# One matmul for mean and variance, and later places for residual, final addition, points and pooled copies

## The chip, the cores and the metric

The kernel runs on one core of a Trainium2 chip. A core has five engines that run side by side, each with its own stream of instructions in order: TensorE (PE, matrix products and transposes), VectorE (DVE, elementwise work and sums), ScalarE (ACT, activations and copies), GpSimd (POOL, which here only issues gathers) and SyncE (SP, which here only issues other transfers). They meet through semaphores: an instruction waits until a counter has reached a number. The metric is the time of one execution on the device in microseconds (us); lower is better.

## What is computed

Two residual layers on a batch of 16 images of 64 channels and 64x64 pixels, all in float32. `_gn` is a group norm with 32 groups, so each group is a pair of channels.

```python
x = x + _L0_conv_ref(_gn(x), ...)   # layer 0
x = x + _L1_conv_ref(_gn(x), ...)   # layer 1

# layer 0: a depthwise convolution whose kernels are made from the image itself
xh = _conv1x1(x, w_in, b_in)                       # 64 -> 128 channels
pooled = jnp.mean(xh, axis=(2, 3))
hcx = jax.nn.relu(pooled @ kg_w1.T + kg_b1)
kernels = (hcx @ kg_w2.T + kg_b2).reshape(b, c, K, K)
y = conv_general_dilated(x_r, k_r, ...)            # 3x3, one kernel for each channel
y = y * jnp.tanh(jax.nn.softplus(y))
return _conv1x1(y, w_out, b_out)                   # 128 -> 64 channels

# layer 1: a deformable 3x3 convolution
offset = _conv2d(x, w_off, b_off)
mask = jax.nn.sigmoid(_conv2d(x, w_mask, b_mask))
xd = _deform_conv(x, offset, mask, w_def)          # 9 taps, each bilinear over 4 corners
cat = jnp.concatenate([xd, offset, mask], axis=1)
z = jnp.einsum('bihw,oi->bohw', cat, w_1x1[:, :, 0, 0]) + ...
return jax.nn.silu(z * inv + ...)                  # batch norm, then silu
```

## The kernel before

**Groups and taps.** The 4096 pixels of an image are worked off in 8 groups of 512 (here "group 0" to "group 7"; the code's `g`). In each group the deformable convolution has 9 taps (`k`). For each tap GpSimd issues 4 gathers that fetch the four corners of 512 points from a table in DRAM (`patch_table`) into a slot of `gat`; VectorE multiplies the slot by its weights (L1096) and adds the four corners (`add_corners`, L1081); TensorE transposes the sums of two taps at a time into `tap_ps` (`transposes`, L545, "pair 0" to "pair 3", and the single ninth tap); ScalarE copies them to `val` (L801); TensorE multiplies them by the weights into `z_ps` (`product`, L553 and L555); ScalarE applies the silu (L810, into `zs`, a part of the tile `n_z`); and VectorE adds the input (`finish`, L1107), whose result SyncE stores (`store_out`). GpSimd may run ahead by less than a group: before taps 0, 2, 4, 6 and 7 it waits for the transposes of the group before (`THROTTLE`), and before each group for its indices `ixu` (L777).

**What goes on beside it.** While image b is gathered, layer 0 of image b+1 and the head of layer 0 of image b+2 are computed in the gaps. Groups 0 to 3 hold the depthwise convolution of b+1 on VectorE (`convolve 0` to `2`, L968 and L971), exp, ln and tanh on ScalarE, and in the following group the 1x1 product `project` (on VectorE L981, on TensorE L464) and the addition of x (`residual`, L995). Group 4 holds both group norms: the one of b+2 (`x_mean`, `x_var`, `x_norm`) with its way to the nine kernel values (`hidden_units`, `kernels`, ending in `kb`, L934), and the one of b+1 (`group_mean`, `group_var`, `normalise`). Groups 5 and 6 make the table and the offsets of b+1 (`to_table`, `offsets`, `to_pixels`; most of it on TensorE, then ScalarE), and group 7 makes the points, indices and corner weights from them (`points 0` to `2`, L1037 to L1057, and `next_indices`), and `hidden 0` to `3` of b+2 (VectorE normalises x into `n_z`, L898; TensorE multiplies by `w_in`, L442; ScalarE copies into `xh`, L689).

**What sets the order.** No scheduler: tuples called PLAN_... give, for each kind of group, pairs of a number and a step. `group()` runs the taps up to that number and then the step, and the same plan is walked by TensorE, ScalarE and VectorE, each with its own function of that name. So (4, "residual") means: after tap 3, on each engine that has a residual step. KK is 9, the end of the group. PLAN_FIRST is group 0, PLAN_BLOCK0 groups 1 to 3, PLAN_NORM group 4, PLAN_PREPARE groups 5 to 7, and PLAN_START the first three groups of the first image. Since every stream is in order, a step that waits holds up all that stands behind it on its engine.

**The lines that the change touches.** The variance of a pair of channels is made from the two channels' own means and variances: TensorE averages the means (L404, L468, one column), VectorE squares the deviation and adds the channel's own variance (L920, L1008), TensorE averages that (L409, L472), and ScalarE takes the root (L670, L726). After group 7 stood `finish(b, NCH - 1)`, outside any plan. Two loads of x stand in SyncE's stream at an image's end and the next one's start (L283).

## Time and profile before

| | us |
|---|---|
| median of 3 runs | 6700.41 |
| lowest and highest | 6698.43, 6706.16 |
| the profiled execution | 6738.33 |
| its span | 6736.5 |
| one image in steady state (image 7) | 418.8 |

The times are those of the whole execution. The profile is of one other execution, 38 us (0.6%) longer than the median. Times on the trace count from the span's start. A row of a timeline gives start, duration, engine, line, operation, tiles (written <- read), shapes, how many instructions are merged, and in brackets how long the engine had been idle before it and what ended that ("remote" and "issue" stand where the profile can't name the one that released it). A matmul in float32 shows as two records. The ends of TensorE's records are modelled, so when a product was really there is read from the engine that waited for it.

### The profile page before, as it was taken

To read this page: it belongs to the slowest core of one execution; us is meant where nothing else is said; L and a number is where in the kernel's file an instruction comes from. 1 tells how busy PE (TensorE), PEld (TensorE's weight loads), DVE (VectorE), ACT (ScalarE), POOL (GpSimd) and SP (SyncE) were. 2 spreads that over 40 slices of the span, in tenths; PEclk is the share of its full clock that TensorE was granted. 3 is DMA by queue.
4 is the path that set the end of the run, shared out by engine and by line. 5 is a ranking of instruction groups with operands and counts; after the bars stand their busy time and mean duration, and the time that the engine had idled before them with its cause. 6 is when DMAs were issued, how large, how long until landed. Compare 5 with 4: busy or idle time off the path is not lost.

```text
span 6736.5 us, 27541 instructions
## 1 busy us (share of the span) xinstructions
PE 3015.6 (45%) x7284; PEld 1087.0 (16%) x7284; DVE 5001.0 (74%) x4373; ACT 1678.4 (25%) x2375; POOL 4385.1 (65%) x4614
## 2 busy tenths in 40 slices
PE   7454353634535344363443635436353353534422
PEld 3121121211112111121111212112121111211100
DVE  5967769587686877768768696776958769587555
ACT  3332222322222222232222222222232222222200
POOL 2666666666666666666666666666666666666666
PEclk8775575755657566575665756657575576756655
DMA  3233343333433333333333333334333343333332
GB/s 90 91 103 113 93 122 96 104 109 97 116 94 105 106 102 113 94 105 110 103 109 96 105 111 101 112 94 119 98 100 112 96 119 94 106 100 103 100 99 88
DMA packets 306947, 695.25 MB, mean 103 GB/s; under 512 B 79172, under 2 KB 148580, under 8 KB 304548
## 3 DMA queue, kind: packets, MB, share of 16 engines
q0 software_dynamic: 221184, 604.27, 29.6%
q1 hardware_dynamic: 85606, 89.22, 5.3%
q8 instruction: 57, 0.93, 0.1%
q14 instruction: 100, 0.82, 0.0%
HBM read 639.06 MB, written 54.12 MB: 103 GB/s over the span
## 4 chain that ended last, share of the span: by engine, by line
DVE 38%; another core or an unknown queue 21%; issue 14%; PE 13%; POOL 7%; ACT 6%; DMA 0%; DVEq 0%; ACTq 0%; POOLq 0%; SPq 0%
DVE pairs L1081 11%; DVE gat L1096 9%; DVE conv_ps L971 8%; POOL gat L381 7%; PE conv_ps L519 3%; PE z_ps L553 2%; PE yo_ps L519 2%; DVE single L1081 1%; PE tap_ps L545 1%; DVE xb L995 1%; DVE stat L997 1%; DVE stat L908 1%; DVE conv_ps L968 1%; DVE uc L974 1%
## 5 line engine op out<-in xcount | busy, mean ns | idle before, releaser
L381 POOL DMA_INDIRECT gat<-patch_table,ixu x4608 | 4377.5, 950 | 2334.9 <-issue 1355.2
L1081 DVE TENSOR_REDUCE pairs<-gat 128x256 f32<-128x1024 f32 x1024 | 1935.3, 1890 | 0.0
L1096 DVE TENSOR_TENSOR gat<-gat,wgt_ps 128x1024 f32<-128x1024 f32 x1152 | 1395.1, 1214 | 515.8 <-DMA gat<-patch_table,ixu 471.6
L545 PE MATMUL tap_ps<-ident,pairs 128*128 128x128 f32 x2048 | 498.3, 388 | 2086.7 <-DVE pairs L1081 1358.9
L553 PE MATMUL z_ps<-val,w_pair 128*64 128x512 f32 x1024 | 895.1, 972 | 680.2 <-ACT val L801 457.4
L801 ACT ACTIVATE val<-tap_ps 128x512 f32<-128x512 f32 x512 | 304.1, 596 | 2742.2 <-remote 1446.5
L545 PEld LDWEIGHTS tap_ps<-ident,pairs 128*128 128x128 f32 x2048 | 329.3, 195 | 2519.1 <-DVE pairs L1081 1569.5
L971 DVE SCALAR_TENSOR_TENSOR conv_ps<-xh,kb,conv_ps 128x1024 f32<-128x1024 f32 x480 | 617.6, 1287 | 12.7
L519 PE MATMUL conv_ps<-np,w_om 128*41 128x512 f32 x732 | 384.0, 681 | 0.0
L519 PE MATMUL yo_ps<-np,w_om 128*41 128x512 f32 x804 | 370.1, 611 | 17.1 <-ACT omc L757 10.2
L555 PE MATMUL z_ps<-cat,w_last 105*64 105x512 f32 x256 | 194.0, 851 | 222.1 <-ACT cat L805 140.7
L553 PEld LDWEIGHTS z_ps<-val,w_pair 128*64 128x64 f32 x1024 | 136.9, 190 | 837.6 <-ACT val L801 487.8
L1081 DVE TENSOR_REDUCE single<-gat 128x256 f32<-128x1024 f32 x128 | 242.8, 1897 | 0.0
L810 ACT ACTIVATE n_z<-z_ps,bn_shift,bn_scale 64x512 f32<-64x512 f32 x128 | 99.0, 774 | 536.7 <-remote 353.6
L1037 DVE TENSOR_TENSOR pt<-px,grid 128x576 f32<-128x576 f32 (+2 forms) x20 | 12.8, 639 | 279.2 <-issue 245.6
L1107 DVE TENSOR_TENSOR n_z<-n_z,xb 64x512 f32<-64x512 f32 x128 | 86.5, 676 | 160.3 <-ACT n_z L810 121.5
L805 ACT ACTIVATE cat<-tap_ps 64x256 f32<-64x256 f32 x256 | 96.7, 378 | 384.4 <-remote 238.7
L898 DVE TENSOR_SCALAR n_z<-xb,mr 64x512 f32<-64x512 f32 x128 | 71.0, 580 | 140.5 <-remote 79.2
L981 DVE TENSOR_TENSOR uc<-uc,conv_ps 128x1024 f32<-128x1024 f32 x60 | 73.0, 1216 | 113.8 <-issue 113.8
L528 PE MATMUL xh_ps<-ident,omc 41*128 41x41 f32 x504 | 54.8, 268 | 215.5 <-ACT omc L759 213.4
L442 PE MATMUL xh_ps<-n_z,w_in 64*128 64x512 f32 x120 | 113.4, 1043 | 81.1 <-issue 45.9
L519 PEld LDWEIGHTS yo_ps<-np,w_om 128*41 128x41 f32 x804 | 94.8, 120 | 272.2 <-issue 254.6
(181 smaller groups left out, 3153.8 us busy)
## 6 DMA issues: line engine op xcount, KB each, us to landing
gat<-patch_table,ixu POOLq DMA_INDIRECT x4608
xb<-in_x SPq DMA_DIRECT2D x31, 1024.0 KB
patch_table<-rec SPq DMA_DIRECT2D x120, 256.0 KB
out<-n_z SPq DMA_DIRECT2D x128, 128.0 KB
patch_table<-np SPq DMA_DIRECT2D x2, 1072.5 KB
patch_table<-gat SPq DMA_DIRECT2D x8, 256.0 KB
patch_table<-rec_l SPq DMA_DIRECT2D x16, 97.0 KB
xb<-in_x SPq DMA_DIRECT2D x2, 512.0 KB, 5.1
```

The lines of the kernel that those rows point to most:

```text
L381: pool.indirect_dma_start(gat[:, slot, t * 2 * REC:(t + 1) * 2 * REC], None, table_rows, bass.IndirectOffsetOnAxis(ixu[:, i, k, t:t + 1], ...
L442: pe.matmul(hidden_ps(n, j)[:, :], w_in[C:, :], n0[C:, j, :], start=True, stop=True).then_inc(xh_mm, 1)
L519: m = pe.matmul((om_ps, yo_ps)[j][0:OM, :], w_om[:, i, :], inner(np1, 0, 128, c * ROWS + 2 * (i // 3), i % 3), start=(i == 0), stop=(i == 5))
L545: m = pe.transpose(tap_ps[p % 2][:, t * 128:(t + 1) * 128], pairs[:, p, t, :] if p < PAIRS else single[:, t, :], ident[:, :])
L553: pe.matmul(z_ps[0:C, :], w_pair[:, p, :], val[:, p % 2, :], start=(p == 0), stop=False).then_inc(z_mm, 1)
L555: pe.matmul(z_ps[0:C, :], w_last[:, :], cat[0:C + OM, b % 2, span(g)], start=False, stop=True).then_inc(z_mm, 1)
L801: act.activation(val[:, p % 2, :], tap_ps[p % 2][:, :], ACT.Copy).then_inc(tap_done, 1)
L805: act.activation(cat[0:C, b % 2, span(g)].rearrange("p (t h x) -> p t h x", h=2, x=128)[:, :, h, :], tap_ps[PAIRS % 2][C * h:C * h + C, 0: ...
L810: act.activation(zs[:, :], z_ps[0:C, :], ACT.Silu, bias=bn_shift[:, :], scale=bn_scale[:, :]).then_inc(zs_done, 1)
L971: dve.scalar_tensor_tensor(acc, src, kb[:, k:k + 1], acc, ALU.mult, ALU.add).then_inc(conv_sum, 1)
L1081: dve.tensor_reduce(total, gat[:, slot(q, k), :].rearrange("p (t d c) -> p t c d", t=TILES, d=4), mybir.AxisListType.X, ALU.add).then_inc( ...
L1096: dve.tensor_tensor(patch, patch, wk.unsqueeze(2).to_broadcast([128, TILES * 4, C]), ALU.mult).then_inc(scaled, 1)
```

## The change

- The averaging matmul takes two columns, mean and variance, in one (`x_mean`, `group_mean`). VectorE adds the square of the deviation to the averaged variance, and ScalarE takes the root of VectorE's result without a second matmul. TensorE's `x_var` and `group_var` are gone.
- `residual` stands after tap 4 and no longer after tap 3, in groups 1 to 3 of all images but the first groups of the first one.
- `finish` of the group before stands at the end of a group and no longer before tap 8; the one of group 7 stands before tap 8 of the next image's group 0 and no longer at the end of group 7. ScalarE's silu waits for the `finish` of the group before.
- In group 7 the order is hidden 0, points 0, hidden 1, points 1 and next_indices, hidden 2, points 2, hidden 3, and no longer points first and hidden after.
- `convolve 0` of group 0 stands one tap earlier.
- In group 4 ScalarE's copies to `pooled` and `hcx` stand one place later under names of their own, and `group_var` behind `hidden_units`.
- SyncE issues the load of x's lower half after the store of the last group, in the next image, and the load of the upper half before it; `to_table 0` has its two waits in the other order.

```diff
-PLAN_FIRST = ((2, "convolve 0"), (3, "convolve 1"), (5, "convolve 2"), (6, "exp"), (7, "ln"), (7, "x_stats"), (8, "tanh"))
-PLAN_BLOCK0 = ((1, "project"), (2, "convolve 0"), (3, "convolve 1"), (4, "residual"), (5, "convolve 2"), (6, "exp"),
-               (7, "ln"), (7, "x_stats"), (8, "tanh"), (8, "finish"))
+PLAN_FIRST = ((1, "convolve 0"), (3, "convolve 1"), (5, "convolve 2"), (6, "exp"), (7, "ln"), (7, "x_stats"),
+              (8, "tanh"), (8, "finish"))
+PLAN_BLOCK0 = ((1, "project"), (2, "convolve 0"), (3, "convolve 1"), (5, "residual"), (5, "convolve 2"), (6, "exp"),
+               (7, "ln"), (7, "x_stats"), (8, "tanh"), (KK, "finish"))
...
-    ((1, "points 0"), (2, "points 1"), (2, "next_indices"), (3, "points 2"), (4, "hidden 0"), (5, "hidden 1"),
-     (6, "hidden 2"), (7, "hidden 3"), (8, "finish")),
+    ((2, "hidden 0"), (3, "points 0"), (4, "hidden 1"), (5, "points 1"), (5, "next_indices"), (6, "hidden 2"), (7, "points 2"), (8, "hidden 3"),
+     (KK, "finish")),
...
+                if b > 0:
+                    store_out(b - 1, NCH - 1)
+                    if b < B - 1:
+                        load_x(b + 1, 0)
...
-                if load:
-                    load_x(b + 2, 0)
...
-                pe.matmul(steps_ps(n)[:, MEAN:MEAN + 1], pair2[C:, :], aggr0[C:, 0:1], start=True, stop=True).then_inc(kernel_pe, 1)
-
-            def x_var(n):
-
-                pe.wait_ge(kernel_dve, n * KERNEL_STEPS + 4)
-                pe.matmul(steps_ps(n)[:, VAR:VAR + 1], pair2[C:, :], sq0[C:, :], start=True, stop=True).then_inc(kernel_pe, 1)
+                pe.matmul(steps_ps(n)[:, MEAN:VAR + 1], pair2[C:, :], aggr0[C:, 0:2], start=True, stop=True).then_inc(kernel_pe, 1)
...
             def x_var(n):
-                act.wait_ge(kernel_pe, n * 5 + 2)
-                act.activation(std0[:, :], steps_ps(n)[:, VAR:VAR + 1], ACT.Sqrt, bias=eps_c[:, :]).then_inc(kernel_act, 1)
+                act.wait_ge(kernel_dve, n * KERNEL_STEPS + 4)
+                act.activation(std0[C:, :], sq0[C:, :], ACT.Sqrt, bias=eps_c[C:, :]).then_inc(kernel_act, 1)
...
                 act.wait_ge(z_mm, q * GROUPS + (GROUPS + 2))
+                act.wait_ge(oc_done, q + 1)
                 act.activation(zs[:, :], z_ps[0:C, :], ACT.Silu, bias=bn_shift[:, :], scale=bn_scale[:, :]).then_inc(zs_done, 1)
...
-                finish(b, NCH - 1)
```

In VectorE's stream the second half of a group 7 stood like this before. `pt<-px,grid` is the first instruction of points 0, `idx<-fl,base` the end of points 1, `n_z<-xb,mr` is a hidden step, `n_z<-n_z,xb` is a finish, and a tap is `gat<-gat,wgt_ps` and `pairs<-gat`:

```order
L898 TENSOR_SCALAR n_z<-xb,mr 64x512 x2
L1096 TENSOR_TENSOR gat<-gat,wgt_ps 128x1024
L1081 TENSOR_REDUCE pairs<-gat 128x4x64
L1107 TENSOR_TENSOR n_z<-n_z,xb 64x512
L1096 TENSOR_TENSOR gat<-gat,wgt_ps 128x1024
L1081 TENSOR_REDUCE pairs<-gat 128x4x64
L1081 TENSOR_REDUCE single<-gat 128x256
L1107 TENSOR_TENSOR n_z<-n_z,xb 64x512
L1090 COPY wgt_ps<-wgt 128x144
L1096 TENSOR_TENSOR gat<-gat,wgt_ps 128x1024 x2
```

and of the change the same engine at the start of that group:

```order
L1080 COPY wgt_ps<-wgt 128x144
L1086 TENSOR_TENSOR gat<-gat,wgt_ps 128x1024 x2
L1071 TENSOR_REDUCE pairs<-gat 128x4x64
L888 TENSOR_SCALAR n_z<-xb,mr 64x512 x2
L1086 TENSOR_TENSOR gat<-gat,wgt_ps 128x1024
L1071 TENSOR_REDUCE pairs<-gat 128x4x64
L1027 TENSOR_TENSOR pt<-px,grid 128x576
```

The first hidden step and two more taps now stand ahead of points 0, which had only the multiplication of tap 0 ahead of it; and the second `n_z<-n_z,xb` at the group's end is gone from there.

ScalarE, from the silu of group 6 (`n_z<-z_ps`) on, before:

```order
L810 ACTIVATE n_z<-z_ps,bn_shift,bn_scale 64x512
L777 ACTIVATE ixu<-idx 128x36
L801 ACTIVATE val<-tap_ps 128x512
L689 ACTIVATE xh<-xh_ps,vec 128x8x64
L689 ACTIVATE xh<-yo_ps,vec 128x8x64
L801 ACTIVATE val<-tap_ps 128x512
```

and now:

```order
L800 ACTIVATE n_z<-z_ps,bn_shift,bn_scale 64x512
L678 ACTIVATE xh<-xh_ps,vec 128x8x64
L678 ACTIVATE xh<-yo_ps,vec 128x8x64
L790 ACTIVATE val<-tap_ps 128x512
L678 ACTIVATE xh<-xh_ps,vec 128x8x64
L678 ACTIVATE xh<-yo_ps,vec 128x8x64
L790 ACTIVATE val<-tap_ps 128x512
L766 ACTIVATE ixu<-idx 128x36
```

The copy of the next image's first indices, which GpSimd waits for, now stands behind two hidden steps and two pairs of taps.

## Rows read from the trace of the kernel before

**Rows 1.** The page's part 1: busy time, share of the span, instructions.

```profile
PE 3015.6 (45%) x7284; PEld 1087.0 (16%) x7284; DVE 5001.0 (74%) x4373; ACT 1678.4 (25%) x2375; POOL 4385.1 (65%) x4614
```

**Rows 2.** The page's part 5: busy us, mean ns | idle before, releaser.

```profile
L1081 DVE TENSOR_REDUCE pairs<-gat 128x256 f32<-128x1024 f32 x1024 | 1935.3, 1890 | 0.0
L1096 DVE TENSOR_TENSOR gat<-gat,wgt_ps 128x1024 f32<-128x1024 f32 x1152 | 1395.1, 1214 | 515.8 <-DMA gat<-patch_table,ixu 471.6
...
L1037 DVE TENSOR_TENSOR pt<-px,grid 128x576 f32<-128x576 f32 (+2 forms) x20 | 12.8, 639 | 279.2 <-issue 245.6
L1107 DVE TENSOR_TENSOR n_z<-n_z,xb 64x512 f32<-64x512 f32 x128 | 86.5, 676 | 160.3 <-ACT n_z L810 121.5
```

**Rows 3.** Waits of the whole span: total us, times, longest.

```profile
ACT val L801 <- remote: 1446.5, 146, 25.0
...
DVE mr L917 <- remote: 180.7, 13, 20.7
...
DVE xb L995 <- remote: 101.9, 32, 19.5
```

**Rows 4.** Windows of image 7: whole, groups 0, 4, 7; PE, PEld, DVE, ACT, POOL busy, clock, DMA.

```profile
3052.50:3471.30 418.80, 183.92 (x448) 66.06 (x448) 313.29 (x270) 105.50 (x148) 276.60 (x292) 0.64 0.35 104
3052.50:3093.50 41.00, 8.81 (x21) 3.72 (x22) 40.59 (x32) 6.43 (x7) 28.52 (x31) 0.50 0.58 150
...
3243.60:3310.90 67.30, 23.52 (x66) 11.81 (x64) 38.32 (x42) 11.03 (x16) 42.52 (x45) 0.58 0.30 92
3381.90:3471.30 89.40, 49.39 (x116) 16.20 (x116) 43.19 (x48) 25.30 (x42) 59.72 (x64) 0.68 0.35 103
```

**Rows 5.** Timeline of VectorE, group 7 of image 7.

```profile
3407.29 0.76 DVE L1037 TENSOR_TENSOR pt<-px,grid 128x576 f32<-128x576 f32 x1 [17.89 <-issue]
...
3442.17 0.55 DVE L898 TENSOR_SCALAR n_z<-xb,mr 64x512 f32<-64x512 f32 x1 [6.64 <-remote]
3447.10 0.55 DVE L898 TENSOR_SCALAR n_z<-xb,mr 64x512 f32<-64x512 f32 x1 [4.38 <-remote]
...
3470.68 0.68 DVE L1107 TENSOR_TENSOR n_z<-n_z,xb 64x512 f32<-64x512 f32 x1 [4.84 <-ACT n_z L810]
3471.29 0.30 DVE L1090 COPY wgt_ps<-wgt 128x144 f32<-128x144 f32 x1
```

**Rows 6.** Timeline of ScalarE, group 7 of image 7: silu of group 6.

```profile
3425.12 0.78 ACT L810 ACTIVATE n_z<-z_ps,bn_shift,bn_scale 64x512 f32<-64x512 f32 x1 [2.06 <-PE z_ps L555]
```

**Rows 7.** Timeline of ScalarE, group 7 of image 6: silu, then hidden copies.

```profile
3016.96 0.77 ACT L810 ACTIVATE n_z<-z_ps,bn_shift,bn_scale 64x512 f32<-64x512 f32 x1 [9.05 <-remote]
...
3027.55 0.69 ACT L689 ACTIVATE xh<-yo_ps,vec 128x512 f32<-128x512 f32 x1 [1.02 <-PE yo_ps L442]
3029.26 0.69 ACT L689 ACTIVATE xh<-xh_ps,vec 128x512 f32<-128x512 f32 x1 [1.02 <-PE xh_ps L442]
```

**Rows 8.** Timeline of VectorE, group 7 of image 6.

```profile
2993.54 0.76 DVE L1037 TENSOR_TENSOR pt<-px,grid 128x576 f32<-128x576 f32 x1 [17.23 <-issue]
...
3051.90 0.68 DVE L1107 TENSOR_TENSOR n_z<-n_z,xb 64x512 f32<-64x512 f32 x1 [10.94 <-ACT n_z L810]
```

**Rows 9.** Timeline of GpSimd: the first gather of image 8.

```profile
3432.51 0.95 POOL L381 DMA_INDIRECT gat<-patch_table,ixu  x1 [0.30 <-issue]
```

**Rows 10.** Timeline of VectorE, group 2 of image 7: residual.

```profile
3170.79 0.75 DVE L995 SCALAR_TENSOR_TENSOR xb<-xh_ps,vec,xb 128x512 f32<-128x512 f32 x1 [11.38 <-remote]
```

**Rows 11.** Timeline of TensorE and VectorE, group 4 of image 7: norm chain.

```profile
3272.57 0.16 DVE L917 COPY mr<-conv_ps 64x1 f32<-64x1 f32 x1 [19.92 <-remote]
3273.23 0.58 PE L409 MATMUL conv_ps<-sq,pair 64*128 64x1 f32 x2 [19.80 <-DVE mr L917]
...
3310.69 0.17 DVE L934 TENSOR_TENSOR kb<-conv_ps,kg_b 128x9 f32<-128x9 f32 x1 [8.53 <-remote]
```

**Rows 12.** Windows between two hidden products, in image 6 and in image 7.

```profile
3025.90:3029.30 3.40, 3.40 (x5) 1.22 (x5) 2.21 (x3) 1.37 (x3) 2.79 (x3) 0.50 0.37 116
3442.20:3447.10 4.90, 2.04 (x2) 0.50 (x2) 0.52 (x2) 0.66 (x2) 3.68 (x5) 0.50 0.33 103
```

More of the change, by code:

```diff
@@ L59 @@
+    ((1, "project"), (2, "convolve 0"), (3, "convolve 1"), (5, "residual"), (5, "convolve 2"), (6, "exp"), (6, "first_points 4"),
+     (7, "ln"), (7, "x_stats"), (8, "tanh"), (KK, "finish")),
+)
+PLAN_NORM = ((1, "project"), (1, "x_mean"), (3, "x_var"), (4, "residual"), (4, "group_mean"), (5, "x_norm"), (6, "pooled"), (6, "hidden_units"),
+             (6, "group_var"), (7, "hcx"), (7, "kernel_taps"), (8, "normalise"), (KK, "kernels"), (KK, "finish"))
 PLAN_PREPARE = (
@@ L862, in image @@
                     steps["x_var"] = lambda b, g, i: x_var(b + 2)
-                    steps["x_norm"] = lambda b, g, i: x_norm(b + 2)
-                    steps["hidden_units"] = lambda b, g, i: hidden_units(b + 2)
+                    steps["pooled"] = lambda b, g, i: x_norm(b + 2)
+                    steps["hcx"] = lambda b, g, i: hidden_units(b + 2)
                 if b == 0:
@@ L1200, in _ @@
             image(B - 1, False, False)
+            finish(B - 1, NCH - 1)
 def kernel(**inputs):
```

54 lines of the change are left out of this document (21 added, 33 removed).

## The prediction

> **What bounds the kernel now.** The shares of busy time come first. VectorE is busy 74% of the span, GpSimd 65%, TensorE 45% [rows 1], so no engine is the bound all the time. The window of one image says the same: 418.8 us, in which VectorE works 313.3 [rows 4]. GpSimd's bound is below that too: a gather takes 0.95 us and the next starts 0.30 later [rows 9], so the 288 gathers of an image need 360 us. What is left is a loop in which the engines wait for each other, and the question is where VectorE, the busiest, stands idle for something that is not a gather. Idle time behind missing gathers is 472 us in the whole span [rows 2]; those gaps cost nothing of their own, for there GpSimd or the release of its slots is late.
>
> The windows by group show the rest. In groups 0 to 3 VectorE hardly waits. Group 4, the two norms, takes 67.3 us with 38.3 of work, and group 7 takes 89.4 with 43.2 of work [rows 4]. So 29 + 46 us of the 105 that VectorE idles in this image lie in two of eight groups, and these are waits of its own: in group 7 for the points' input (279 us in 20 steps over the span) and for the silu ahead of `finish` (121 us in 13 waits) [rows 2], in group 4 for the averaged mean (181 us in 13 waits) [rows 3]. In groups 1 to 3 there is one such wait, `residual` (102 us in 32 waits) [rows 3].
>
> Behind most of them is TensorE, in a way that its busy share hides. Between two hidden products ScalarE's copies stand 3029.26 - 3027.55 = 1.71 us apart in image 6 [rows 7], but VectorE, which waits for the same products, gets them 3447.10 - 3442.17 = 4.93 us apart in image 7 [rows 5]. The granted clock is 0.50 in both stretches, the lower of the two levels (1.2 GHz) [rows 12]. So products arrive late, at a third of the pace, for a reason other than the clock, and ScalarE waits 1446 us in 146 pieces for releases that the profile can't name [rows 3]. (The Trainium skill, "TensorE: Matmul & The Clock Gate", section "What's actually happening", knows two states, half rate and full rate; by that rule a product would never take longer than 1.71 us here, image 7's group 7 would look like image 6's, and the sum below would be the fast case alone. The trace disagrees.)
>
> **Group 7, step by step.** I call P the start of points 0 and F the silu of group 6, with which TensorE is through with group 6.
>
> Image 6, the usual pattern: P at 2993.5, F at 3016.96, last `finish` at 3051.9 [rows 7, 8]; with its own 0.6 the next image starts 59.0 us after P. Image 7, with late products: P 3407.3, F 3425.1, next image 3471.3, so 64.0 us after P and 46.2 after F [rows 5, 6]. In all 13 images from 1 to 13 the stretch from P is 56.8 to 64.5 us, so these two stand for them.
>
> Work in the group is 43.2 us [rows 4]. A tap is 1.21 + 1.89 us less the overlap of their ends, some 2.95 [rows 2]. Before P stands one multiplication; now two full taps, the third, hidden 0 and the copy of the weights stand there, 10 us, of which VectorE has time for all: it waits 17.2 and 17.9 us for P today [rows 5, 8]. The last `finish` (0.6) leaves. So after P there are 43.2 - 0.6 - 10.1 = 32.5 us of work left. Of these, points 0 (4.0) and one tap follow at once, 7 us. Then a **new wait**: hidden 1 needs hidden 0's product, which is in TensorE's stream behind all of group 6, so it comes at about F + 1.7 and F + 3.4. Today this wait is small because three points parts and three taps stand ahead of it. With F - P = 23.4 (image 6) VectorE idles some 16 us there. After hidden 1's own 1.0, at F + 4, 24.6 us remain, and the next image begins at F + 28.6, which is P + 52.0 against 59.0: **7.0 us saved**. In image 7 hidden 1's product is late, by today's times 22.0 us after F (3447.1) [rows 5, 6]; hidden 2 waits for it, and behind it 15.6 us of work remain: F + 37.6 against 46.2, 8.6 saved. I take 7.0 for 14 images: **98 us**. So most of the 17 + 9 us that the two waits promise is not had: it comes back as the wait for hidden 0.
>
> The cover: convolve 0 of the next group now follows closely, and needs hidden 3's copy. VectorE is there 8.6 us after hidden 3's normalisation (a tap, the single sum, finish, the weights and one multiplication). Two products at 1.71 fit under that, two at 4.93 and a copy of 0.69 don't: up to 2 us, and more if one is queued; 4 us in the four images or so with late products, **-16 us**. GpSimd: today its first gather for image 8 starts 7.4 us after F [rows 6, 9], its indices being copied right behind F. Now the copy stands behind hidden 0, hidden 1 and points 1: F + 10.5 with fast products, so 3 to 4 us later. VectorE starts the group at F + 28.6, and needs the last gather of the group some 36 us later, F + 65; GpSimd delivers it at F + 11 + 45 + 4 = F + 60 (36 gathers of 1.25 [rows 9], and 4 to land, an estimate). The 5 us of slack cover it; without them the excess counts in full. The load of x's lower half, now 35 us later, has from there to group 1's `residual`, some 35 us; the slack stays.
>
> **Residual.** One tap later, each wait shrinks by up to 2.95 us. 102 us in 32 waits over the span, 11.4 the largest in image 7 [rows 3, 10]; about one wait above 3 us an image, and smaller ones. By the ends: nothing, if the product comes only so much later; 32 x 2.95 = 94 if each wait held a tap. I take **50**, nearer to the one full tap an image (15 x 2.95 = 44).
>
> **The norms.** Two one-column matmuls an image go. The record shows 0.58 us [rows 11]. The mean's wait (19.9 us in image 7) is not touched: it stands before the removed step, and behind it VectorE and TensorE go on within 0.7 us [rows 11]. What goes is a round trip in which ScalarE's root waited for TensorE. Bounds: 0 where VectorE does not wait for the root, as in image 7; one late product, 4.93 x 2 an image, at the other end. Nearest are the rows of image 7: I take 1 us an image, **15 us**. The wait for `kb` at the group's end (8.5 us) [rows 11] stays, for its nine products stay; `pooled`, `hcx` and `group_var` on ScalarE hardly change their neighbours. (What the record of TensorE says here is weak evidence, and the Trainium skill, "Perfetto Trace Analysis", section "Tensor Engine Instruction", says that the profiler estimates its end; the 4.93 us above agree.)
>
> `finish` at the end of groups 1 to 6 costs nothing: the silu it waits for is over by then, and the silu that now waits for it needs products of the same group's last tap. The convolve 0 that stands earlier moves work, no more.
>
> **Sum.** 98 + 50 + 15 - 16 = 147 us, against the profiled execution 6738.3 - 147 = 6591, and against the median, 0.6% lower, 6700 - 147 = 6553. I say 6555 us.
>
> **Rivals.**
> - **All is kept** (0.12). If TensorE reaches hidden 0 before F matters, because its late releases thin out when hidden steps are spread, group 7 saves the silu wait (9 us) and the three taps under P (9 us): 18 an image, 252, with residual 50 and norms 15 gives 6700 - 317 = 6383; with half the effect 6460. For it: late products are not tied to the clock [rows 12]. Against: F - P is 18 to 23 us in most images and group 6 itself is not changed.
> - **The gain is swallowed** (0.11). VectorE comes earlier to the waits of groups 1 to 4, all on TensorE's late products; if these come by TensorE's own time, the waits grow by what was gained. Then 6690 to 6700, no change. This is also the case in which the change doesn't do what its parts say. Against: in image 7 TensorE too waits 19.8 us for VectorE [rows 11].
> - **The first gathers starve the next image** (0.15, slower). The next indices now need four hidden products, two sets of transposes and their copies. At 4.93 us each this is 30 us. Today a group 0 after a usual group 7 ends at F + 35.5 + 41.0 = F + 76.5 [rows 4, 7, 8]; gathers started at X end it at X + 53 (45, landing, and the last tap's work). It decides at X = F + 23.5; today it is F + 7.4 [rows 6, 9]. At X = F + 31 each image loses 7.5 us, 105 in 14, less the 65 from residual and norms, and VectorE then runs without any lead, in which each of its later waits blocks GpSimd too; I price this at half of those 102 us: 6700 + 40 + 51 = 6790. For it: late products in groups 7 of several images [rows 5]. Against: even in image 7 hidden 1 was through at F + 22.
>
> **How the numbers follow.** Forecast 0.62, rivals 0.12, 0.11 and 0.15. The forecast's own range is 6450 to 6645: residual from 0 to 94, norms 0 to 60, the new convolve wait 0 to 40. The range of 8 in 10 leaves out half of the first rival and most of the last: 6450 to 6710. A measurement of this kernel tells about 0.2%, 13 us, from no change. Faster by more: 0.62 + 0.12 + 0.03 of the swallowed case and 0.01 of the last, less 0.02 of the forecast: 0.76. Within 0.2%: 0.09. Slower: 0.15.
>
> **What would show it.** Right: the wait ahead of points 0 falls from 17 to some 8 us and `finish` has no wait in group 7; a wait of 10 to 17 us stands before the second hidden step (L888); the next image begins 50 to 56 us after P; GpSimd's first gather comes 10 to 14 us after F. Residual's waits fall by half. Wrong: the stretch from P stays at 59 (the wait for hidden 0 is longer than F allows), VectorE waits for gathers in group 0, convolve 0 waits over 5 us, or group 4 grows by what group 7 lost.

## The result and the profile after

The changed kernel takes 6723.1 us (median of 6 runs, 6711.8 to 6738.6), the kernel before on the same chip 6702.9 (6 runs). The ratio is 1.0028, 95% interval 1.0015 to 1.0041: **slower by 0.3%**. The prediction said 6555 us, with 6450 to 6710 as its range. The profiled execution took 6711.8 us (span 6710.0); that of before took 6738.3, which is 0.5% above its median, so differences of less than 1% between the two profiles say nothing about the total. The ratios do.

The page's part 1, and from part 5 (busy us, mean ns | idle before, releaser) the gathers, VectorE's multiplication, ScalarE's copy of a pair, and VectorE's product of `project`:

```profile
PE 2993.6 (45%) x7220; PEld 1076.5 (16%) x7220; DVE 4997.5 (74%) x4373; ACT 1677.8 (25%) x2375; POOL 4397.9 (66%) x4614
...
L385 POOL DMA_INDIRECT gat<-patch_table,ixu x4608 | 4390.3, 953 | 2295.9 <-issue 1351.0
L1086 DVE TENSOR_TENSOR gat<-gat,wgt_ps 128x1024 f32<-128x1024 f32 x1152 | 1396.9, 1214 | 670.2 <-DMA gat<-patch_table,ixu 625.8
L790 ACT ACTIVATE val<-tap_ps 128x512 f32<-128x512 f32 x512 | 303.1, 596 | 2652.0 <-remote 1641.6
L971 DVE TENSOR_TENSOR uc<-uc,conv_ps 128x1024 f32<-128x1024 f32 x60 | 73.0, 1217 | 223.0 <-issue 215.6
```

Busy times are within 1% of those of before. VectorE's idle time has moved: ahead of the multiplication of gathered data it grew from 516 us [rows 2] to 670. The list of waits over the span (total us, times, longest) has, for the places of [rows 3], a wait of ScalarE's copy that grew by 195 us and two of VectorE that hardly changed; L985 is `residual`, L907 the averaged mean, L888 the hidden step:

```profile
ACT val L790 <- remote: 1641.6, 162, 23.6
...
DVE mr L907 <- remote: 180.3, 11, 21.5
...
DVE xb L985 <- remote: 107.9, 27, 27.1
...
DVE n_z L888 <- remote: 41.0, 8, 18.3
```

The windows of image 7, whole and its groups 0, 4 and 7 (columns as in [rows 4]):

```profile
3035.70:3436.50 400.80, 180.81 (x446) 64.19 (x444) 313.37 (x270) 104.40 (x147) 272.24 (x286) 0.64 0.37 107
3035.70:3077.30 41.60, 13.06 (x29) 4.68 (x28) 41.19 (x33) 10.65 (x14) 31.55 (x34) 0.54 0.55 146
3236.70:3308.70 72.00, 24.23 (x63) 11.38 (x63) 38.33 (x41) 17.36 (x22) 43.91 (x47) 0.57 0.29 87
3381.50:3436.50 55.00, 40.41 (x99) 13.60 (x97) 42.53 (x47) 17.23 (x28) 39.96 (x42) 0.75 0.37 112
```

Group 7 takes 55.0 us where it took 89.4. One image is not the mean, though. Taken from one copy of the weights on VectorE to the next (L1080; L1090 before) and averaged over images 1 to 13, the groups are, in us:

```
group             0     1     2     3     4     5     6     7    image
before          41.0  49.6  48.5  47.6  67.9  28.1  46.0  84.1   412.8
after           46.2  55.8  52.7  54.8  66.5  27.7  46.4  61.4   411.5
```

**Group 7 gives 22.7 us an image, three times what was forecast, and groups 0 to 3 take back 22.8.** VectorE's idle time alone, from all its rows of the same images, tells where:

```
group             0     1     2     3     4     5     6     7    image
before           0.4   4.4   3.3   2.5  29.5   0.6  17.8  41.0    99.5
after            4.9  10.5   7.5   9.7  28.1   0.3  18.3  19.2    98.5
```

Of the 22.0 us by which groups 0 to 3 idle longer, 11.9 stand ahead of `project` (L971), which waits for ScalarE's tanh, and the tanh stands in ScalarE's order behind copies of the pairs; 4.7 are behind gathers, 3.4 ahead of convolve 0 and 1.8 ahead of `residual`.

The table by group for GpSimd, from the first gather of a group to the first of the next, hardly changes in any column:

```
group             0     1     2     3     4     5     6     7    image
before          48.2  54.3  51.4  48.2  53.0  51.2  54.5  51.8   412.7
after           49.8  50.4  51.4  50.6  52.5  50.4  54.4  51.7   411.1
```

VectorE now starts an image 12 us behind GpSimd's first gather of it; before it was 34. It has moved closer to the gathers, and the image is no shorter for it.

Group 7 of image 6 on VectorE, to be read beside [rows 7, 8]:

```profile
2990.18 0.76 DVE L1027 TENSOR_TENSOR pt<-px,grid 128x576 f32<-128x576 f32 x1 [1.61 <-issue]
...
3004.44 0.56 DVE L888 TENSOR_SCALAR n_z<-xb,mr 64x512 f32<-64x512 f32 x1 [7.23 <-remote]
3008.64 0.55 DVE L888 TENSOR_SCALAR n_z<-xb,mr 64x512 f32<-64x512 f32 x1 [3.64 <-PE xh_ps L441]
...
3035.68 0.29 DVE L1080 COPY wgt_ps<-wgt 128x144 f32<-128x144 f32 x1
```

with ScalarE's silu of group 6 and its copy of the next indices, and GpSimd's first gather for image 7:

```profile
3001.64 0.77 ACT L800 ACTIVATE n_z<-z_ps,bn_shift,bn_scale 64x512 f32<-64x512 f32 x1 [5.52 <-remote]
...
3020.10 0.24 ACT L766 ACTIVATE ixu<-idx 128x36 int32<-128x36 int32 x1
```

```profile
3021.20 0.94 POOL L385 DMA_INDIRECT gat<-patch_table,ixu  x1 [6.89 <-ACT ixu L766]
```

So P is 2990.2, F is 3001.6, the wait ahead of points 0 is 1.6 us, hidden 1 waits 7.2 + 3.6 us for hidden 0's product, the next image starts at P + 45.5 = F + 34.0, and GpSimd's first gather at F + 19.6. Image 6 is one of six of the 13 with such a wait; in the other seven no hidden step waits, and the next image starts at P + 34 to 35.

### The profile page after: what moved, and what is told of

Read it like the earlier page. It is cut to its first block, busy times and chain, and to the rows that moved or that the text cites. A ratio compares the mean times of both kernels' runs of the same rounds, so it can differ in the third digit from the quotient of the medians.

```text
span 6710.0 us, 27541 instructions
## 1 busy us (share of the span) xinstructions
PE 2993.6 (45%) x7220; PEld 1076.5 (16%) x7220; DVE 4997.5 (74%) x4373; ACT 1677.8 (25%) x2375; POOL 4397.9 (66%) x4614
## 4 chain that ended last, share of the span: by engine, by line
DVE 33%; another core or an unknown queue 21%; issue 15%; POOL 12%; PE 12%; ACT 6%; DMA 1%; DVEq 0%; POOLq 0%; ACTq 0%; SPq 0%
POOL gat L385 12%; DVE pairs L1071 10%; DVE gat L1086 8%; DVE conv_ps L961 6%; PE conv_ps L514 4%; PE yo_ps L514 2%; PE z_ps L548 2%; DVE single L1071 1%; DVE xb L985 1%; DVE stat L987 1%; PE z_ps L550 1%; ACT val L790 1%; PE tap_ps L540 1%; DVE uc L964 1%
## 5 line engine op out<-in xcount | busy, mean ns | idle before, releaser
L540 PE MATMUL tap_ps<-ident,pairs 128*128 128x128 f32 x2048 | 480.2, 380 | 1388.7 <-DVE pairs L1071 894.9
L514 PE MATMUL yo_ps<-np,w_om 128*41 128x512 f32 x804 | 364.3, 603 | 12.3 <-ACT omc L746 11.9
L550 PE MATMUL z_ps<-cat,w_last 105*64 105x512 f32 x256 | 210.1, 917 | 319.6 <-ACT cat L794 184.0
L971 DVE TENSOR_TENSOR uc<-uc,conv_ps 128x1024 f32<-128x1024 f32 x60 | 73.0, 1217 | 223.0 <-issue 215.6
L907 DVE COPY mr<-conv_ps 64x1 f32<-64x1 f32 x14 | 2.3, 161 | 207.6 <-remote 180.3
L888 DVE TENSOR_SCALAR n_z<-xb,mr 64x512 f32<-64x512 f32 x128 | 66.9, 557 | 99.4 <-remote 41.0
L745 ACT ACTIVATE omc<-yo_ps,vec 32x512 f32<-32x512 f32 x67 | 45.4, 677 | 373.3 <-remote 231.5
```

The source lines that it names most:

```text
L514: m = pe.matmul((om_ps, yo_ps)[j][0:OM, :], w_om[:, i, :], inner(np1, 0, 128, c * ROWS + 2 * (i // 3), i % 3), start=(i == 0), stop=(i == 5))
L540: m = pe.transpose(tap_ps[p % 2][:, t * 128:(t + 1) * 128], pairs[:, p, t, :] if p < PAIRS else single[:, t, :], ident[:, :])
L550: pe.matmul(z_ps[0:C, :], w_last[:, :], cat[0:C + OM, b % 2, span(g)], start=False, stop=True).then_inc(z_mm, 1)
```

## The experiments

Ratios are to the kernel before in the same job, with the 95% interval. The jobs were on different chips (the kernel before took 6703 to 6751 us), so only ratios are compared across them. "Held" is GpSimd's idle time beyond the 0.30 us between two gathers, for each of the images 1 to 13. "Latency" is the time from the end of VectorE's second sum of a pair to the start of ScalarE's copy of it, averaged over the four pairs of groups 0 to 3; in good time it is 1.2 us, and I call it late above 3 us. Both are worked out from all such rows of one profiled execution.

**The parts of the change, alone and in pairs.** e1 has the norms' single matmul, e2 only the order of group 7, e3 only the last `finish` in the next image's group 0, e4 both of these:

```diff
@@ e2
-    ((1, "points 0"), (2, "points 1"), (2, "next_indices"), (3, "points 2"), (4, "hidden 0"), (5, "hidden 1"),
-     (6, "hidden 2"), (7, "hidden 3"), (8, "finish")),
+    ((2, "hidden 0"), (3, "points 0"), (4, "hidden 1"), (5, "points 1"), (5, "next_indices"), (6, "hidden 2"), (7, "points 2"), (8, "hidden 3"),
+     (8, "finish")),
@@ e3, with store_out and load_x of SyncE moved behind it, and ScalarE's silu waiting for the finish before
-PLAN_FIRST = ((2, "convolve 0"), (3, "convolve 1"), (5, "convolve 2"), (6, "exp"), (7, "ln"), (7, "x_stats"), (8, "tanh"))
+PLAN_FIRST = ((2, "convolve 0"), (3, "convolve 1"), (5, "convolve 2"), (6, "exp"), (7, "ln"), (7, "x_stats"), (8, "tanh"), (8, "finish"))
```

> The kernel before with only the merged norm matmuls (two one-column matmuls an image less, ScalarE's root straight from VectorE). Theory S (TensorE's late products swallow what VectorE gains): ratio 0.997 to 1.003, since nothing on TensorE's long stretches goes. Rival R (the parts of the change have effects of opposite sign that cancel): this is one of the gaining parts, 15 to 60 us, ratio 0.991 to 0.998.

Measured 1.0012 (0.9996 to 1.0028). The norms' part is worth nothing that can be told from zero.

> The kernel before with only group 7's new order (hidden 0, points 0, hidden 1, points 1, hidden 2, points 2, hidden 3); the last finish stays at the end of group 7 and the other finish steps stay before tap 8. Theory S: group 7 gets shorter by 5 to 15 us an image and groups 0 to 4 longer by as much, ratio 0.996 to 1.004. Rival R: this part gains by itself, 7 us x 14 = 98 us as the prediction had it, or more, ratio 0.97 to 0.986.

Measured 1.0084 (1.0055 to 1.0113): by itself group 7's order **costs** 0.8%. Its group 7 is 86.4 us, not shorter: the wait ahead of points 0 falls from 17 to 4 us an image, and the wait ahead of the last `finish` grows from 9 to 18.5. Held rises from 52.6 to 56.4 us.

> The kernel before with only the last finish of an image moved before tap 8 of the next image's group 0, with its store, the load of x's lower half behind it and ScalarE's wait; the other finish steps stay where they were. Theory S: the wait of 5 to 12 us ahead of it goes, convolve 0 or a later step waits instead, ratio 0.997 to 1.003. Rival R: 9 us x 15 = 130 us gained, ratio 0.98, if this is a gaining part.

Measured 0.9990 (0.9980 to 0.9999). Group 7 falls by 10.5 us to 73.6, and groups 0 to 4 grow by 8.5; image 412.0.

> Both parts together: group 7's new order and the last finish in the next image. Theory S: group 7 falls from 84 to about 60 us as in the change, groups 0 to 4 grow by 20, ratio 0.997 to 1.006. Rival R: if the loss of the change sits in its other parts (residual, convolve 0, finish at the group's end), the gain of 24 us x 14 shows at least in half: ratio 0.95 to 0.975.

Measured 1.0074 (1.0045 to 1.0102): group 7 falls to 64.3 us, groups 0 to 3 grow from 186.7 to 209.7, VectorE's lag behind the first gather is 14 us. This is the whole picture of the change, made by these two edits, and they lose. What they lose beyond the change's own 1.0028, the rest gives back: norms, `residual`, convolve 0, and the `finish` steps of groups 1 to 6 at the group's end. The last of these was not run alone.

**Is it GpSimd's release?** My first theory was that GpSimd is held by TensorE's late transposes, and that releasing it earlier would give the time back. e5 releases each tap's gathers by VectorE's sum (VectorE then waits for the transposes before it overwrites a pair); e6 keeps three buffers of indices and copies them a group earlier; e7 is both on the kernel before, e8 both on the changed one.

```diff
@@ e5, GpSimd
-                            if k in THROTTLE:
-                                pool.wait_ge(tap_mm, q * GROUPS + THROTTLE[k])
+                            if k < KK - 1:
+                                pool.wait_ge(summed, q * KK + k + 1)
@@ e5, VectorE, add_corners
+                if k % 2 == 0:
+                    dve.wait_ge(tap_mm, q * GROUPS + (k // 2 + 1))
@@ e6
-        ixu = sb("ixu", [128, 2, KK, TILES], I32)
+        ixu = sb("ixu", [128, 3, KK, TILES], I32)
```

> The kernel before, but GpSimd's gather for a slot waits for VectorE's sum of that slot in the group before (summed) and no longer for TensorE's transposes of it; VectorE waits for those transposes instead before it overwrites a pair. Theory G (GpSimd's loop sets the time: 360 us of gathers an image plus some 52 us in which it is held, and it is held since TensorE's products and transposes come late): the time that GpSimd is held falls by the part that hangs on transposes, 10 to 25 us an image, ratio 0.94 to 0.98. Rival V (VectorE's own waits set the time): GpSimd only runs further ahead, ratio 0.997 to 1.003.

Measured 1.1008 (1.0986 to 1.1029), 10% **slower**. Held rises to 99 us an image, and the mean latency in groups 5 and 6 from 26 to 43 us (the second pair of group 6: 78 us on average).

> The kernel before with three index buffers and ScalarE's copy of the indices one group earlier, from the second image on, so that it no longer stands right behind a late silu. Theory G: the first gather of a group is held less (some 30 of the 52 us an image lie ahead of a group's first gather), unless the transposes' release comes last there too; ratio 0.95 to 0.99. Rival V: 0.997 to 1.003.

> The kernel before with both: release by VectorE's sums and indices one group earlier. Theory G: GpSimd is hardly held by TensorE any more, and what is left is VectorE's work in groups 0 to 4 and its waits there; ratio 0.92 to 0.96. Rival V: 0.997 to 1.003.

> The change with both. Theory G: with GpSimd free to run ahead, VectorE's 23 us an image saved in group 7 are kept, so that it is faster than the same edits on the kernel before (e7) by 1 to 4%. Rival V: VectorE's waits for late products grow as they did in the change, and it stays within 1% of e7.

Measured: e6 1.0008 (0.9991 to 1.0024), e7 1.1073 (1.1045 to 1.1102), e8 1.1017 (1.0990 to 1.1044). The theory fell: none of these releases shortens the image. Two things besides the gathers' lead changed, though, so that the 10% is not the price of the lead alone. VectorE's sum of a tap, which waited for nothing before (0.0 [rows 2]), now waits for the transposes: 14 us an image in e5, 39 in e7, 52 in e8. And in e5 most of GpSimd's held time is a wait for the indices, whose copy stands behind late steps on ScalarE (total us over the span, times, longest):

```profile
POOL gat L381 <- ACT ixu L777: 1219.9, 76, 35.3
...
POOL gat L381 <- DVE pairs L1083: 338.2, 118, 21.8
```

That TensorE's steps in groups 5 and 6 come later still is measured; whether by the gathers' lead or by VectorE's new wait is not shown. The next question is whether TensorE is late because of the gathers.

**What makes TensorE late.** e11 is the changed kernel from image 2 on without half of the gathers, and e13 has all of them with half of the bytes (in both the rest of a slot keeps older values, so that the arithmetic stays and its result is another); e12 gives TensorE twelve more products a group; e10 holds GpSimd a pair longer.

```diff
@@ e11, with VectorE's wait adapted
-                            for t in range(TILES):
+                            for t in range(TILES if b < 2 else TILES // 2):
@@ e13
-gat[:, slot, t * 2 * REC:(t + 1) * 2 * REC]
+gat[:, slot, t * 2 * REC:t * 2 * REC + (2 * REC if b < 2 else REC)]
@@ e12, behind product(b, g, k // 2 - 2)
+                            for _ in range(4):
+                                pe.matmul(tap_ps[k // 2 % 2][:, 0:128], ident[:, :], ident[:, :], start=True, stop=True)
@@ e10
-THROTTLE = {0: 1, 2: 2, 4: 3, 6: 4, 7: 5}
+THROTTLE = {0: 2, 2: 3, 4: 4, 6: 5}
```

> The changed kernel from image 2 on without half of the gathers: of the four tiles of a tap only the first two are fetched, the others keep older values; all arithmetic, all waits and TensorE's whole program stay. Theory D: with half of the gather traffic and half of GpSimd's descriptor work TensorE's steps come in time; the mean latency from VectorE's sum to ScalarE's copy in groups 0 to 3 falls from 11 us to 2 or less, ScalarE's waits for TensorE fall below half, and the time to what VectorE has to do, about 5000 to 5400 us. Theory I (TensorE is late where it has little work to do, whatever the gathers do): the latencies in groups 0 to 3 stay at 8 us or more, and the time falls only by VectorE's waits for gathers, 32 us of 411 an image, to about 6300 us.

Measured 5321.9 us, ratio 0.7885 (0.7871 to 0.7900). In images 2 to 13, which lack the gathers, an image takes 317.5 us and not 411.6, the latency is 1.2 us on average where the changed kernel has 11.3, and 1 of 192 pairs is late and not 122; in groups 5 and 6, where TensorE makes the table and the offsets, it is 10.9 and not 24.5. Part 1, and from part 5 the gathers, VectorE's multiplication and ScalarE's copy:

```profile
PE 2761.9 (52%) x7220; PEld 1020.9 (19%) x7220; DVE 4978.5 (94%) x4373; ACT 1675.7 (32%) x2375; POOL 2472.0 (47%) x2598
...
L385 POOL DMA_INDIRECT gat<-patch_table,ixu x2592 | 2464.4, 951 | 2810.4 <-PE tap_ps L540 1866.4
...
L1086 DVE TENSOR_TENSOR gat<-gat,wgt_ps 128x1024 f32<-128x1024 f32 x1152 | 1392.6, 1212 | 68.4 <-DMA gat<-patch_table,ixu 57.8
L790 ACT ACTIVATE val<-tap_ps 128x512 f32<-128x512 f32 x512 | 305.0, 596 | 2041.6 <-PE tap_ps L540 1721.0
```

VectorE is busy 94% of the span, and in images 2 to 13 it idles 5.5 us an image. The word that changes is the releaser of ScalarE's copy: it was "remote", a release that no record of TensorE fits in time, and is TensorE's own transpose now. The end of a group shows the size of it. First VectorE's last sum in e11, at the end of group 2 of image 8, and the ScalarE copies and silu that follow from it, then the same steps in the changed kernel, at the end of image 7:

```profile
3004.42 1.90 DVE L1071 TENSOR_REDUCE single<-gat 128x256 f32<-128x1024 f32 x1
```

```profile
3005.70 0.60 ACT L790 ACTIVATE val<-tap_ps 128x512 f32<-128x512 f32 x1 [1.86 <-PE tap_ps L540]
3008.21 0.78 ACT L794 ACTIVATE cat<-tap_ps 64x256 f32<-64x256 f32 x2 [1.92 <-PE tap_ps L540]
3010.98 0.77 ACT L800 ACTIVATE n_z<-z_ps,bn_shift,bn_scale 64x512 f32<-64x512 f32 x1 [0.68 <-issue]
```

```profile
3434.05 1.92 DVE L1071 TENSOR_REDUCE single<-gat 128x256 f32<-128x1024 f32 x1
```

```profile
3446.44 0.60 ACT L790 ACTIVATE val<-tap_ps 128x512 f32<-128x512 f32 x1 [9.89 <-remote]
3457.64 0.78 ACT L794 ACTIVATE cat<-tap_ps 64x256 f32<-64x256 f32 x2 [10.61 <-issue]
3468.84 0.77 ACT L800 ACTIVATE n_z<-z_ps,bn_shift,bn_scale 64x512 f32<-64x512 f32 x1 [10.42 <-issue]
3479.34 1.09 ACT L790 ACTIVATE val<-tap_ps 128x512 f32<-128x512 f32 x2 [9.60 <-remote]
```

From the end of the last sum to the silu it is 4.7 us in e11 and 32.9 in the changed kernel, where the steps come 11.2, 11.2 and 10.5 us apart. That is a long one: at the end of group 7 the changed kernel has 4.8 to 36.8 us, 20.7 on average, and e11 has 4.6 in each of images 2 to 13.

How the gathers do it is less simple than the averages look. The last of the four steps above ends at 3479.34, and GpSimd had by then stood idle since 3471.1:

```profile
3480.06 0.94 POOL L385 DMA_INDIRECT gat<-patch_table,ixu  x1 [8.95 <-remote]
```

In groups 0 to 3 of images 1 to 13 of the changed kernel GpSimd idles at the moment of the copy in 78 of the 134 late pairs and in none of the 74 others. (It often waits for those very transposes.) So a gather that is being issued at the moment is not what makes a step late.

> The changed kernel from image 2 on with the same 288 gathers an image, each of them fetching only the first half of its rows (64 KB, not 128 KB); the other half keeps older values. GpSimd has as much to issue, the DMA engines move half. If the number of gathers sets the time (GpSimd's 360 us an image) and their bytes make TensorE late: the latencies from VectorE's sum to ScalarE's copy in groups 0 to 3 fall from 11 us to 3 or less, held time falls from 50 us to 30 or less, time 6100 to 6450. If neither GpSimd's issue nor TensorE's lateness depends on bytes: latencies 8 us or more, held 45 to 55, time within 1% of 6740. If GpSimd's time for a gather falls with the bytes (0.95 us busy and 0.3 us of issue each now), the time goes towards the 5322 us of the half as many gathers.

Measured 1.0060 (1.0043 to 1.0077). The DMA share falls from 0.36 to 0.23, and nothing else moves: latency 10.8 us, late in 67%, held 56.1. The bytes are not the cause; that leaves the number of gathers, GpSimd's work for them, or the room that fewer gathers leave in the whole loop. (The Trainium skill, "DMA: Bandwidth & Descriptors", section "Anatomy of one DMA — SWDGE (gpsimd) path", gives such a DMA a fixed part of some 2.0 us and a part by bytes; by its fit, an estimate, half of 128 KB would save 0.15 us of 2.3. The profile has no time of landing for a gather, so no run here shows that sum; GpSimd's own 0.95 us a gather is another figure, and it did not change.)

> The changed kernel with 12 more products of 128 columns in each group on TensorE (4 behind each of three products of the sample's pairs, about 0.5 us each, 6 us a group, 48 us an image; their results are not used). Theory I (TensorE is late where it is idle): the mean latency in groups 0 to 3 falls below 5 us and the time falls by 1% or more. Theory D (gathers): the latency stays at 11 us or grows by the 2 us of each block, and the time is the same or up to 1% longer; if each product completes late by itself, as dependent steps do (4.9 to 5.6 us apart), the time grows by several per cent.

Measured 1.0052 (1.0037 to 1.0068). TensorE's mean granted clock rises from 0.63 to 0.69 (the levels are 1.2 and 2.4 GHz), its busy time over 13 images by 15%, and 64% of the pairs are late as before; latency 8.8 us, by pair 6.8, 3.0, 9.0 and 16.6. A clock and a busy share raised by this much make no fewer pairs late; larger steps were not tried.

> The changed kernel with GpSimd held one pair of taps longer: the gather of tap 0 waits for the second of TensorE's pairs of the group before (it was the first), tap 2 for the third, tap 4 for the fourth, tap 6 for the fifth. Theory D (TensorE completes late because gathers run without pauses): GpSimd's held time rises from 50 us an image to 70 or more, the mean latency from VectorE's sum to ScalarE's copy in groups 0 to 3 falls from 11 us to below 6, and the time falls or stays (6680 to 6720). Theory L (the gathers need every bit of lead, lateness has another cause): the latency stays near 11, VectorE's wait for gathers grows by the 10 us a group that the lead shrinks by where lead is short (groups 0, 6, 7), and the time grows by 2 to 5% (6850 or more).

Measured 1.0299 (1.0284 to 1.0315). Held rises to 65.7 us, the latency falls to 8.0, and VectorE waits 54 us an image for gathers and not 32. The latency lies between my two numbers and the time went as theory L had it, so the loop can't be bought off this way.

**What VectorE's time in group 7 is worth.** e14 puts eight more instructions into group 7 of the changed kernel, behind the last hidden step.

```diff
+                for _ in range(8):
+                    dve.tensor_scalar(uc[...], np_runs[:, 0:2 * CH], 20.0, None, ALU.min).then_inc(padded, 1)
```

> The changed kernel with eight more instructions of 1.2 us on VectorE in group 7 of each image behind its last hidden step (9.8 us an image, 137 us in all; their results are not used). Theory P (GpSimd's issue and its held time set the image; VectorE has slack in group 7): VectorE's wait for gathers and for products in groups 0 to 3 shrinks by about what group 7 grows, lag of the gathers in group 0 grows from 12 us to about 20, and the time grows by 0.5% at most. Theory V (VectorE's path sets it, as the prediction had it): the time grows by most of 137 us, 1.5 to 2%: ratio to the kernel before 1.018 or more.

Measured 1.0046 (1.0030 to 1.0062). The eight took less than I had reckoned, 5.8 us in one row:

```profile
3055.28 5.79 DVE L1098 TENSOR_SCALAR uc<-np 128x1024 f32<-128x1024 f32 x8
```

So some 87 us were added (5.8 in each of 15 images). Against the change the time grew by 0.18% of 6747, 12 us, and by the two intervals at most 0.47%, 32 us. Groups 0 to 3 fell from 209.5 to 198.8 us and group 7 grew from 61.4 to 74.5. Most of VectorE's added work in group 7 costs nothing: the exchange between group 7 and groups 0 to 3 runs the other way as readily.

The windows from image 1's start to image 14's, 13 images, show what does count. In this order: before, after, e2, e14, e10, e5; the fifth pair of numbers is GpSimd's busy time and its instructions:

```profile
574.46:5940.49 5366.03, 2406.73 (x5824) 865.70 (x5824) 4072.11 (x3486) 1368.75 (x1924) 3559.07 (x3745) 0.63 0.36 105
```

```profile
553.26:5902.82 5349.56, 2384.73 (x5774) 852.75 (x5772) 4068.91 (x3485) 1369.87 (x1927) 3573.33 (x3749) 0.63 0.36 105
```

```profile
583.34:6007.72 5424.38, 2395.94 (x5824) 863.81 (x5824) 4069.73 (x3486) 1371.59 (x1924) 3571.46 (x3758) 0.63 0.36 104
```

```profile
576.98:5974.97 5397.99, 2388.26 (x5773) 848.72 (x5772) 4139.91 (x3590) 1367.13 (x1924) 3568.15 (x3741) 0.63 0.36 104
```

```profile
581.91:6118.06 5536.15, 2421.97 (x5773) 855.67 (x5772) 4073.73 (x3485) 1368.28 (x1924) 3559.22 (x3745) 0.63 0.35 101
```

```profile
644.43:6602.43 5958.00, 2450.33 (x5824) 870.34 (x5824) 4061.36 (x3486) 1372.54 (x1924) 3550.81 (x3744) 0.62 0.32 94
```

GpSimd's busy time is 3551 to 3573 us in all six, and with the 0.30 us between gathers (3744 x 0.30 = 1123) 4674 to 4696, or 360 us an image. The rest of the image is held time: 412.8 = 360 + 53, 411.5 = 361 + 50, 417.3 = 360 + 56, 415.2 = 361 + 54, 425.9 = 360 + 66, 458.3 = 360 + 99. This sum holds by its making, since GpSimd is either issuing or held; it does not say what sets the held time. What it teaches is where a gain must show: a change that leaves the held time alone leaves the image alone, whatever VectorE does.

**The rest of the change, and a better version.** e9 is the changed kernel with group 7's earlier order, e16 the same with GpSimd's fifth wait at tap 8 and not at tap 7; e15 is the kernel before with the later residual alone; e17 and e18 are the changed kernel with residual and with convolve 0 put back.

```diff
@@ e15 (e17 is the reverse)
-(3, "convolve 1"), (4, "residual"), (5, "convolve 2")
+(3, "convolve 1"), (5, "residual"), (5, "convolve 2")
@@ e18
-PLAN_FIRST = ((1, "convolve 0")
+PLAN_FIRST = ((2, "convolve 0")
@@ e16
-THROTTLE = {0: 1, 2: 2, 4: 3, 6: 4, 7: 5}
+THROTTLE = {0: 1, 2: 2, 4: 3, 6: 4, 8: 5}
```

> The changed kernel with the earlier order in group 7 alone (points 0 to 2 in units 1 to 3, then the hidden steps); residual, norms, convolve 0 and the last finish stay as changed. Group 7's new order by itself cost 0.8% on the kernel before, and the order with the last finish moved 0.7%; the whole change 0.3%. If these add up, this kernel takes 6670 to 6685 us (ratio to the kernel before 0.995). If group 7's new order works only together with the rest (the last finish moved, the residual later), this kernel is no faster than the change: 6720 us or more, ratio 1.003 or above. In the first case groups 0 to 3 sum to about 188 us as before (changed kernel: 209.5), and group 7 takes 74 us, as with the last finish moved alone.

Measured 0.9983 (0.9974 to 0.9992): the fastest version. Three (e3, e9 and the next, e16) lie below the kernel before by more than their intervals leave, and none by more than 0.17%. Groups 0 to 3 sum to 197.5 us, between my two numbers; group 7 is 73.6.

> The changed kernel with the earlier order of group 7 (0.9983 by the run before) and GpSimd's fifth wait one tap later: taps 6 and 7 go out on TensorE's fourth pair of the group before, and the wait for its fifth stands at tap 8. Theory P with lateness from gathers: GpSimd gets four gathers (5 us) further ahead at most; its held time at tap 7 (0.8 us an image and group at most) goes, and the time stays within 0.3% of 0.9983; a gain above 0.5% would say that the release by TensorE's last pair was a limit of its own, a loss above 0.5% that even this little lead makes TensorE later.

Measured 0.9989 (0.9981 to 0.9998), held 51.9 us; no gain over e9.

> The kernel before with the residual one unit later in groups 0 to 3 (from unit 4 to unit 5) and nothing else. The prediction put this at 50 us, ratio 0.9925. From the differences so far (the whole change 1.0028, group 7 and the finish together 1.0074, norms 1.0012) the residual and convolve 0 together gave 0.4 to 0.5%: expected here 0.996 to 0.998. If the residual gives nothing by itself, the ratio is within 0.1% of 1.

Measured 0.9997 (0.9986 to 1.0007). The later residual gives nothing.

> The changed kernel with the residual back at unit 4 in groups 1 to 3 and at the start. If the residual's place matters only where the gathers come late (group 0 to 3 of the changed kernel, lead 12 us and not 34), this is slower than the change: 1.005 to 1.007. If it matters nowhere, the ratio stays 1.0028 within 0.1%.

> The changed kernel with the first third of the convolution in an image's group 0 back at unit 2. If the earlier convolve 0 covers the wait for the first gathers, which the changed kernel has and the kernel before has not, this is slower than the change: 1.005 to 1.007, with VectorE's wait for gathers in group 0 longer. If it is worth nothing, the ratio stays 1.0028 within 0.1%; below 1.002 would say that the earlier place costs, by its wait for TensorE (3.4 us an image).

Measured: e17 1.0039 (1.0025 to 1.0054) and e18 1.0053 (1.0034 to 1.0072), against 1.0028 (1.0015 to 1.0041) for the change. In the changed kernel the earlier convolve 0 is worth about 0.25% and the later residual about 0.1%, and each interval overlaps that of the change, so this split is likely and not shown.

## Why the prediction was wrong

**The step that failed first is in what bounds the kernel.** It worked out GpSimd's 360 us an image, set them against 418.8, and called GpSimd "below that too"; of VectorE's idle time behind gathers it said that it costs nothing of its own. It didn't ask what the missing 53 us are. They are held time, GpSimd has no other slack, and a gain must come out of them. Of the waits of VectorE that it summed (29 + 46 us), 7.0 us an image in group 7, 98 us in all, were priced as coming off the time; the runs show that they don't. VectorE's idle time is 99.5 us an image before and 98.5 after: what group 7 lost, groups 0 to 3 gained. e4 makes this exchange with two edits, and e14 makes it the other way.

**Group 7: mechanism right in part, size wrong, worth wrong.** The new wait ahead of hidden 1 is there in six of the 13 images (7 to 18 us; 7.2 + 3.6 in image 6; forecast 10 to 17 everywhere) and absent in seven. The next image starts at F + 34.0 there and F + 29 in most others (forecast F + 28.6), `finish` waits no more, the wait ahead of points 0 is 3 us (forecast 8). What was mis-sized is F - P: taken as 23.4 from image 6, where the 13 images before average 19.2, it is 11.5 in that image now, about 5 in seven others and 9.2 on average, so the group gives 22.7 us and not 7.0. (By the prediction's own numbers the idle time behind hidden 0 is 52.0 - 32.5 = 19.5 us, not some 16; the 7.0 doesn't hang on it.) Why F comes sooner after P is not shown. And none of it is kept: "the next image begins earlier" was counted as time won. GpSimd starts the next image 24 to 34 us after P, 27.7 on average, where it was 25 to 28, 26.6 on average ([rows 5, 9] have 25.2 for image 7); only VectorE came earlier.

**The cover.** The first gather was put at F + 10.5, with 5 us of slack left in group 0. It comes at F + 19.6 in image 6, because F moved forward and the indices did not. VectorE waits 626 us and not 472 for gathers over the span; an image has 3.7 us more of it in group 7, 3.7 in group 1 and 1.0 in group 0. The 4 us that a gather was given to land are nearer 2.7, from the start of a tap's last gather to the multiplication that waited for it (the middle one of 172 such waits before). Convolve 0's wait was put at 16 us in all. One row of image 6, group 0, alone has half of it:

```profile
2624.78 1.29 DVE L958 TENSOR_SCALAR conv_ps<-xh,kb 128x1024 f32<-128x1024 f32 x1 [7.92 <-issue]
```

It stands in four of the 13 images (7.9 to 13.3 us), 3.4 us an image on average, some 48 over 14; the sign that was named for this ("over 5 us") appeared.

**Residual and norms.** 50 us were forecast for the residual; its waits are 107.9 us in 27 where they were 101.9 in 32 [rows 3], and e15 gives 0.9997. The step "each wait shrinks by up to 2.95 us" took the product's time as fixed; the runs show only that the waits did not shrink. The norms' 15 us would be a ratio of 0.9978, which lies outside e1's interval; a ratio of 1 lies inside it.

**The rivals.** "The gain is swallowed" (0.11) is what happened, in its words: VectorE comes earlier to waits on late steps, and these grow (above all ahead of `project`, by way of ScalarE's tanh). Its price, 6690 to 6700, was near; the result is 23 to 33 us more. The argument against it, that TensorE too waits 19.8 us for VectorE [rows 11], was one row of group 4, and group 4 is just where nothing changed (67.9 and 66.5 us). "The first gathers starve the next image" (0.15) had the direction right and the place wrong: its price needs a first gather at F + 31, it came at F + 18.6 on average and hardly later after P than before, and gathers account for 4.7 of the 22.0 us. (In "All is kept" half of the effect would give some 6510 by its own terms, not 6460.)

**What stays open.** What sets the 50 us of held time is open; that GpSimd's issuing is the limit is argued from the sum, and no run slowed GpSimd's own issuing to test it. Why group 7's order costs and isn't merely free (1.0084 alone) is only argued too: its hidden steps stand among the pairs on TensorE, the latency in group 7 rises from 5.3 to 10.1 us, and GpSimd's held time from 52.6 to 56.4. Through what the gathers make TensorE late isn't settled either: e11 and e13 leave GpSimd's own issuing, the number of its transfers, and the looser loop, and no run here tells these apart. The loading of TensorE's program is an unlikely cause: the changed kernel's page counts 158 packets on its two instruction queues over the whole span, and groups 0 to 3 of 13 images alone have 134 late pairs, the middle one by 15.6 us.

## What to carry to other kernels

Make the sum of busy, issue and held time for every engine that feeds the others, the least busy-looking one included; where all of its slack is held time, only what shortens that is a gain. The sum makes such an engine a candidate for the pace and no more: cutting its work (as e11 did) or padding it tests it. Before counting a wait that goes away, add a few microseconds of work at its place: if the time doesn't move, the wait was slack. And where late completions depend on how fast the loop runs, price a moved step by the loop's own response, not by today's rows.

## What the hardware did that I had not expected

- TensorE's completions are late with many gathers in the loop: at an unchanged stream of TensorE, latency 11.3 us with 288 gathers an image and 1.2 us with 144 (e11), 10.8 with 288 of half the bytes (e13), at mean granted clocks of 0.63, 0.67 and 0.63. By what path is open.
- Late steps come at nearly even distances (11.2, 11.2 and 10.5 us in the rows above), and a clock raised from 0.63 to 0.69 (e12) leaves as many pairs late. The last of them ends 8 us after GpSimd has stopped.
- Letting gathers go out as soon as their slot was free, with VectorE's sum waiting for the transposes in GpSimd's place, made the kernel 10% slower (e5).
